# Layer 0 of a two-layer graph network: two relation rows gathered instead of one in every other quad of edges

## What is computed

```
h_src = h_hc[src];  r_uv = r_hc[edge_type]           # two gathers per edge
m = clifford_linear(h_src * r_uv, msg_w, msg_b)      # linear, so it can follow the sum
m = m * sigmoid(r_uv @ gate_w.T + gate_b) * (deg_src[src] * deg_dst[dst]) ** -0.5
h_agg = segment_sum(m, dst)
x = layernorm(x + clifford_linear(h_hc + h_agg, upd_w, upd_b))
```

## Time and profile before

| | before |
|---|---|
| median of 3 runs | 3801.09 us (3783.49 to 3802.06) |
| the profiled execution | 3782.04 us, its span 3779.7 us |
| granted TensorE clock, mean | 0.911 |
| busy over the span: PE, PEld, DVE, ACT, POOL | 81%, 69%, 66%, 62%, 57% |

### The profile page before, as it was taken

How to read it: one execution, slowest core, us unless ns; L and a number is a source line. 1 busy time by engine, 2 the same in 40 slices (tenths; PEclk the granted TensorE clock), 3 DMA queues, 4 the chain that set the end, 5 groups by cost and what they waited for, 6 DMA issues and landing times. The chain is left out here.

```text
span 3779.7 us, 55957 instructions
## 1 busy us (share of the span) xinstructions
PE 3080.2 (81%) x17027; PEld 2611.1 (69%) x17027; DVE 2509.8 (66%) x5700; ACT 2338.1 (62%) x4157; POOL 2150.0 (57%) x1993
## 2 busy tenths in 40 slices
PE   5468887887878778777759999949999986999985
PEld 4356666666666666666648888847888865777774
DVE  8857777777777777777736565635555654666676
ACT  1066666666666666666548787728777845777761
POOL 5266666666666666666436555555555555555551
PEclk6589999999998998899979999979999988999998
DMA  4245555555454554455456565455555537555552
GB/s 124 82 128 146 136 138 146 139 135 143 132 141 131 141 136 133 132 140 135 118 188 199 171 192 183 149 175 183 175 178 168 179 107 229 189 175 187 177 155 80
DMA packets 345442, 575.72 MB, mean 152 GB/s; under 512 B 44709, under 2 KB 242678, under 8 KB 345142
## 3 DMA queue, kind: packets, MB, share of 16 engines
q1 hardware_dynamic: 249753, 316.82, 27.2%
q0 software_dynamic: 91872, 252.80, 24.1%
q10 hardware_dynamic: 3517, 2.48, 0.2%
HBM read 487.13 MB, written 84.78 MB: 151 GB/s over the span
## 5 line engine op out<-in xcount | busy, mean ns | idle before, releaser
L1484 POOL DMA_INDIRECT rows_arena<-table_h,src_idx x936 | 989.6, 1057 | 858.4 <-DVE row_pairs L1825 515.9
L1484 POOL DMA_INDIRECT rows_arena<-table_scaled_x,src_idx x782 | 889.4, 1137 | 574.4 <-DVEq L1759 333.4
L2053 PE MATMUL bank<-wide_counts,h_pairs 128*128 128x512 f32 (+1 forms) x4704 | 1085.9, 386 | 155.1 <-ACT wide_counts L1633 125.7
L2053 PEld LDWEIGHTS bank<-wide_counts,h_pairs 128*128 128x128 f32 x4704 | 854.5, 194 | 329.5 <-issue 143.1
L1990 PE MATMUL bank<-rel_pairs,ftype_hot 125*128 125x258 f32 x4688 | 758.0, 312 | 53.0 <-issue 53.0
L1833 DVE TENSOR_TENSOR h_pairs<-rows_arena,h_pairs 128x512 fp32r<-128x512 f32 x600 | 399.5, 681 | 528.7 <-ACT h_pairs L1630 394.4
L1990 PEld LDWEIGHTS bank<-rel_pairs,ftype_hot 125*128 125x128 f32 x4688 | 666.7, 204 | 87.6 <-issue 58.7
L1633 ACT CAST wide_counts<-rows_arena 128x1024 fp32r<-128x1024 bf16 (+1 forms) x600 | 634.7, 1058 | 74.4 <-DMA rows_arena<-edge_counts 74.1
L1630 ACT CAST h_pairs<-rows_arena 128x512 fp32r<-128x512 f32 x600 | 367.7, 613 | 354.8 <-PE bank L2053 213.6
L1654 ACT CAST rows_arena<-bank 128x448 bf16<-128x448 f32 (+1 forms) x940 | 426.4, 505 | 259.1 <-remote 98.8
L2039 PE MATMUL bank<-rows_arena 128*128 128x448 bf16 (+1 forms) x940 | 262.5, 363 | 323.1 <-ACT rows_arena L1654 227.1
(11 more groups left out here) (186 smaller groups left out, 3265.5 us busy)
## 6 DMA issues: line engine op xcount, KB each, us to landing
rows_arena<-edge_counts SPq DMA_DIRECT2D x273, 512.0 KB
edge_counts<-fcount SPq DMA_DIRECT2D x60, 832.0 KB
rows_arena<-in_edge_type_dram SPq DMA_DIRECT2D x195, 187.5 KB
rows_arena<-table_h SPq DMA_DIRECT2D x36, 512.0 KB, 12.1
rows_arena<-table_h,src_idx POOLq DMA_INDIRECT x936
rows_arena<-table_scaled_x,src_idx POOLq DMA_INDIRECT x782
table_h<-chunk_info SPq DMA_DIRECT2D x96, 128.0 KB
rows_arena<-edge_counts SPq DMA_DIRECT2D x39, 256.0 KB
```

The costliest lines, as they stand in the source:

```text
L1484: pool.indirect_dma_start(out=rows[:, g % ring, c, :], out_offset=None, in_=table[:, :], in_offset=bass.IndirectOffsetOnAxis(ap=src_idx[:, ...
L2053: last = pe.matmul(bank[2 + h][:, 0:cols_of(w)], h_pairs[:, v % HALVES, part, b % HALF, h * P:(h + 1) * P], wide_counts[:, v % HALVES, b % ...
```

## The change

`POOL_REL` becomes `((0, 1), (0,))`: in quads with an even number (98 of 196) the relation rows of chunks 0 and 1 are gathered, and TensorE selects those of chunks 2 and 3; odd quads stay as they were. So the edge types loaded and the one-hots made for an even quad are those of 256 edges instead of 384, PE makes two relation products instead of three (there, `relation(s,2)` does nothing), and POOL issues six gathers instead of five. The buffer `rel_rows` gets 2 + 1 + 2 + 1 rows for the ring of four quads, with `rel_slot` as its index; the arenas keep their size, since `block_rows` is set by a larger term. `type_hot` keeps its width of 384.

```diff
--- before.py
+++ after.py
@@ -53,7 +53,7 @@
 COUNT_HOTS = 3
 SEG_RING = 1024
 ACT_HOTS = 3
-POOL_REL = ((0,),)
+POOL_REL = ((0, 1), (0,))
 PASSES, PASS_COLS, LAST_COLS = 8, 512, 256
 COUNT_RING, STORE_COLS = 256, 64
 ROW_PAIRS = 2
@@ -160,11 +160,13 @@
         arena = sb("arena", [P, max(DH * AGGW, sum(arena_w.values()))])
         agg = arena[:, 0:DH * AGGW].rearrange("p (h n) -> p h n", h=DH)
 
-        pass0_w = {"rows": RING0 * GC * TW, "msg": 2 * GC * (D + SETW), "rel_rows": RING0 * max(map(len, POOL_REL)) * RW,
+        REL_SLOTS = [len(POOL_REL[i % len(POOL_REL)]) for i in range(RING0)]
+        assert RING0 % len(POOL_REL) == 0
+        pass0_w = {"rows": RING0 * GC * TW, "msg": 2 * GC * (D + SETW), "rel_rows": sum(REL_SLOTS) * RW,
                    "types_i": 3 * GC * P, "types_h": GC * P}
         made_w = max(GC - len(i) for i in POOL_REL) * P
         WORK0 = 4
-        fast_w = {"rows": RING0 * GC * TW, "rel_rows": RING0 * max(map(len, POOL_REL)) * RW,
+        fast_w = {"rows": RING0 * GC * TW, "rel_rows": sum(REL_SLOTS) * RW,
                   "msg": MSGS * GC * (D + 2), "hot": MSGS * GC * WIDE,
                   "type_off": ACT_HOTS * made_w // 2, "vec": 2 * D, "work": WORK0 * D}
         seg_w = {"seg_ring": SEG_RING + WIDE, "types_i": TYPES * made_w, "vT": 2 * D,
@@ -1343,6 +1345,10 @@
             def pool_rel(g):
                 return [c for c in POOL_REL[g % len(POOL_REL)] if c < chunks_of(g)] if first else []
 
+            def rel_slot(g, i):
+
+                return sum(REL_SLOTS[:g % ring]) + i
+
             def made_edges(g):
 
                 return min(E, (GC * g + len(pool_rel(g))) * P), min(E, (GC * g + chunks_of(g)) * P)
@@ -1377,8 +1383,7 @@
                 if first:
                     w_l = wT["msg"]
                     rows = lent_rows("rows", P, fast_w).rearrange("p (r c f) -> p r c f", r=ring, c=GC)
-                    rel_rows = (lent_rows("rel_rows", P, fast_w)
-                                .rearrange("p (r c f) -> p r c f", r=ring, c=max(map(len, POOL_REL))))
+                    rel_rows = lent_rows("rel_rows", P, fast_w).rearrange("p (r f) -> p r f", f=RW)
                     msg = lent_rows("msg", P, fast_w).rearrange("p (r c f) -> p r c f", r=MSGS, c=GC)
                     hot = lent_rows("hot", P, fast_w).rearrange("p (r c w) -> p r c w", r=MSGS, c=GC)
                     types_i = lent_seg("types_i", RP).bitcast(I32).rearrange("p (r e) -> p r e", r=TYPES)
@@ -1488,7 +1493,7 @@
                             for i, c in enumerate(pool_rel(g)):
                                 col = g * GC + c
                                 pool.indirect_dma_start(
-                                    out=rel_rows[:, g % ring, i, :], out_offset=None, in_=table_rel[:, :],
+                                    out=rel_rows[:, rel_slot(g, i), :], out_offset=None, in_=table_rel[:, :],
                                     in_offset=bass.IndirectOffsetOnAxis(ap=type_idx[:, col:col + 1], axis=0),
                                 ).then_inc(s_rows[g % ring], 16)
 
@@ -1747,7 +1752,7 @@
                                 if g >= MSGS:
                                     dve.wait_ge(s_seg, g - MSGS + 1)
                             if c in pool_rel(g):
-                                relation = rel_rows[:, g % ring, pool_rel(g).index(c), 0:D + 1]
+                                relation = rel_rows[:, rel_slot(g, pool_rel(g).index(c)), 0:D + 1]
                             else:
                                 r = products(g) + c - len(pool_rel(g))
                                 dve.wait_ge(s_rel_mm, r + 1)
```

## The result

The changed kernel takes 3890.75 us (median of 4 runs, 3885.23 to 3905.21) where the kernel before takes 3798.09 us in the same comparison (4 runs, 3783.49 to 3802.06): a ratio of 1.0247, 95% interval 1.0214 to 1.0280. The forecast was 3690 us. The profiled execution took 3894.90 us, span 3892.6, mean clock 0.886 (before 0.911). In the changed kernel every line from L1484 on stands 5 lines lower: L1484 is L1489, L1490 is L1495, L1611 is L1616, L1654 is L1659, L1990 is L1995, L2006 is L2011, L2039 is L2044.

A forecast was written before the change was run, and what follows sets the result against it. Layer 0 was taken as bound by a loop of PE's relation products and ACT's one-hots, with DVE third. 127 + 31 + 12 = 170 us, times 0.62, gives 105; 3782 less 105 is 3677, plus 13 is 3690 us, range 3650 to 3765.

The forecast's parts named there:

- What hides it is the 333 us wait for ring places: POOL, layer 0: 98 added gathers, 129 us, fit into its idle wait for free ring places.
- Relation products, 98 x 1.294 = 127 us: PE, layer 0: removing one relation product per even quad shortens the loop by 127 us (109 to 172).
- The factor 0.62: Layer 0: share of the 170 us sum expected as gain, 105 us, the rest lost where DVE's count work comes last.
- rival 2: Layer 0 loop: no change, since waits simply move; 3776 to 3814 us, say 3795; chance 0.10.
- One-hots: ACT, layer 0: one-hots of 256 instead of 384 columns save 31 us (L1611) and 12 us (L1597).
- POOL's own numbers: POOL, layer 0: L1490 x294 at about 1016 ns; ring-place wait falls from 333 to about 100 us.
- No gather is late: DVE, layer 0: idle time before the first message of a quad is 0.0 and stays near 0.
- Contention of POOL and DVE: Layer 0: 98 more gathers run beside DVE; their slowing was taken as already in the 1016 ns mean.
- The forecast of the transfers: DMA, layer 0: added gathers at 0.54 us each make 53 us more, raising DMA from 50% to 53%.
- Rival 3: POOL, layer 0: denser gathers get longer, over 1.25 us on average, making the kernel slower; chance 0.05.
- Rival 1: Layer 0: POOL or DVE becomes the bound, gain only 20 to 60 us, centre 3755 us; chance 0.20.

The follow-up runs named there:

- g1: Kernel before plus four POOL memsets behind the gathers of even quads, no gather added: ratio 1.0078 on chip 1.
- f1: Kernel before plus 98 relation gathers that no message reads, all products kept: ratio 1.0372 on chip 8.
- f2: Changed kernel without its 98 added gathers, so 98 relation products fewer than the kernel before: ratio 0.9973 on chip 8.
- b0: Kernel before, unaltered, run again on chip 11: one run, 3719.7 us.
- e2: Changed kernel without its 98 added gathers, on chip 0: ratio 0.9957 to the kernel before at 3510 us.
- f4: Changed kernel, unaltered, run again on chip 8: ratio 1.0285 to the kernel before at 3743 us.
- h1: Kernel before with no relation gather in odd quads, all four chunks selected there (98 gathers fewer, 98 products more): ratio 1.0029 on chip 8.
- g3: Kernel before without the relation gather of even quads from quad 4 on (96 gathers fewer), products kept: ratio 0.9778 on chip 1.
- e1: Kernel before plus 98 relation gathers that no message reads, on chip 0: ratio 1.0011 to the kernel before at 3510 us.

## Why the prediction failed

**The step that failed** is "What hides it is the 333 us wait for ring places": the 98 gathers were priced at POOL's time and found hidden. POOL's time was in fact nearly hidden (g1: 0.8%), but a gather has a second price, which POOL's time doesn't explain: with more gathers PE's signals reach DVE and ACT late more often (104 long waits in f1, 40 and 52 in the kernel before). Where that shows, 98 gathers cost 139 us (f1), 1.4 us each, all of it on the path. The rows had this: 255 us of waits, summed over ACT and DVE, for "remote" in the earlier trace rows (98.8 + 80.0 + 76.6), the largest item of those that ACT's staging waited for, and I took them for PE and left them unexplained. Asking when these waits end would have put the gathers under suspicion, though no row gave a price.

**Relation products, 98 x 1.294 = 127 us.** They vanish from PE (L1995: 3904 matmuls, as foreseen), but not with 127 us. Busy time falls from 758.0 to 667.4 in the same stretch, 91 us (forecast about 630, so 128), since the clock fell from 0.93 to 0.87 and each matmul that stays takes longer, the sums most of all (392.4 to 430.0 us). L2006 of before (in the stretch of the earlier trace rows) and f2's own rows show it; the last row is b0's, which f2 is compared with below.

```profile
L2006 PE MATMUL bank<-rows_arena 128*128 128x258 f32 x1552 | 392.4, 398 | 0.0
```

```profile
L1995 PE MATMUL bank<-rel_pairs,ftype_hot 125*128 125x258 f32 x3904 | 643.0, 312 | 52.5 <-issue 52.5
L2011 PE MATMUL bank<-rows_arena 128*128 128x258 f32 x1552 | 417.6, 417 | 0.0
L2044 PE MATMUL bank<-rows_arena 128*128 128x448 bf16 (+1 forms) x938 | 267.4, 369 | 364.8 <-ACT rows_arena L1659 238.2 <-issue 88.6 <-DVE rows_arena L1799 32.6
```

```profile
L2039 PE MATMUL bank<-rows_arena 128*128 128x448 bf16 (+1 forms) x938 | 257.4, 357 | 300.3 <-ACT rows_arena L1654 217.1 <-issue 54.2 <-DVE rows_arena L1794 28.0
```

**The factor 0.62** was the second failure. The products alone, with the narrower one-hots, gain 10 us (f2) and 15 us (e2), not 105: a factor of 0.06 to 0.09. In f4's set the two failures make up the whole error: from 105 us of gain to 107 us of loss are 212 us, of which 139 are the gathers and 95 the products, less 22 because the two together cost less than their sum. Of f2's saving (beside b0, another chip: products 750.4 to 643.0, -107 us) the sums give back 27 us (390.4 to 417.6), the count products 10, and the waits before them 65 (300.3 to 364.8). That is rival 2, "waits that simply move", with 0.10; what I had against it, that ACT's chain begins when the products end, came from one stretch of the timeline and didn't hold for the layer. In how many slots it fails I did not count. In the other direction the products do count, by 94 us for 98 (h1 against g3, with other chips between them). So the kernel before seems to stand near the point where PE's products stop being the bound: fewer gain little, more cost three quarters of their length. No run shows this on one chip.

**One-hots.** Sizes were right: 125x256 takes 501 ns (forecast 500) and 510 (515), 294 of each. Their 43 us (31 + 12) are in the same lost sum.

**POOL's own numbers.** L1495 x294 at 1004 ns was right (1016 forecast). The ring wait stayed at 326 us instead of falling to 100, because the layer grew by 128 us, as much as the gathers take. **No gather is late** held: the idle time before the first message is 0.0 in the changed kernel too.

```profile
L1760 DVE TENSOR_TENSOR rows_arena<-rows_arena 128x257 f32<-128x257 f32 x293 | 116.6, 416 | 0.0
```

**Contention of POOL and DVE** did not grow: DVE's L1799 lasts 417/430/653 ns (min/median/max) against 417/430/655 in the earlier trace rows. The rule of the Trainium skill (SBUF — State Buffer, "Who interferes with whom") that I weighed against the change pointed the right way, slower, by a mechanism that these rows don't bear out. The forecast of the transfers had a slip: 53 us more in a layer of 1575 us are 57% of DMA, not 53%; nothing hung on it, and the measured share is 48%.

**Rival 3** ended on the right side with the wrong mechanism: it wanted gathers over 1.25 us with their issue apart, and they are 1.10 us on average, as before. **Rival 1** (POOL full) did not happen here; it is what chip 0 shows (6.5 us of ring waits in e1), and there it costs 4 us.

**Still open.** Why PE's signals are late while gathers run, why on three chips of four, and whether without recording too, no run tells. That a run of gathers ends where the waits do is a coincidence in time; part of it works the other way round, as a DVE that is held back frees no ring place and so makes POOL pause. What is shown by adding and removing is that the number of gather instructions moves the time (0.978, 1, 1.037 for -96, 0, +98, on chips 1 and 8), that bytes, rows and plain transfers don't, and that POOL's time explains a fifth of it (0.8% of 3.7%). That the late signals carry the rest is argued from the long waits, which grow with the gathers, but in f2 (73) and g1 (67) are also more numerous without a gather more.

## What to carry over

Before moving work from an engine to gathers, look at every wait that the profile can't attribute and ask what ends it: here 255 us of "remote" waits stood in the profile beforehand, and with 98 gathers more they grew to 431 (207.6 + 106.8 + 117.0). In a kernel like this one, price a gather by the instruction, not by its rows or bytes nor by the idle time of POOL, and measure on more than one chip. Here an operation on a loop whose engine also waits in it gave back little of its length when it was removed (10 us of 127) and cost most of it when it was added (94 us of 127): take the two as different numbers.

## What the runs showed of the hardware

- PE's signals can reach other engines 10 us after the recorded end of the matmul, several together (1853.71 to 1863.92 us in the changed kernel), while increments of DVE, ACT and the DMAs arrive in between; on chip 0 the gathers-only kernel shows a mean lag of at most 0.03 us, on chip 8 one of 1.49.
- The kernel before takes 3510 us on one chip and 3743 to 3798 us on others, 7 to 8% more. Where the excess lies can be read from the gathers-only kernel, which has a trace on two chips (e1 and f1): layer 0, where most gathers run, takes 1464 and 1829 us, the rest 1846 and 1887.
- A gather of 16 rows occupies POOL for 848 ns at the least, one of 128 rows for 945; the landing comes some 3.6 us after POOL has issued the last of five.
- The granted clock of layer 0 is 0.95 with 96 gathers fewer (g3) and 0.87 in the changed kernel; PE's idle time ahead of the count products is 278 and 471 us in the two. The clock went down as PE's waits grew.
